# Single-row DMAs for two more kinds of chunk: the weighted sum and the sort of a graph network kernel on one core

## The reference, cut to what matters

```python
def _L0_gnn_ref(h, e, src, dst, W, b):          # "wsum": weighted sum of gathered rows
    m = h[src] * e
    ft = jax.ops.segment_sum(m, dst, num_segments=N_NODES)
    return ft @ W.T + b

def _L1_gnn_ref(x, edge_index, edge_attr, u, batch, W1, b1, W2, b2):   # "pool": needs edges by source
    row = edge_index[0]
    seg_sum = jax.ops.segment_sum(edge_attr, row, num_segments=N)
    seg_max = jax.ops.segment_max(edge_attr, row, num_segments=N)
    ...
# then _L2 ("rel": rows of hw[etype, src] summed by dst) and _L3 ("att": softmax over dst, rows z[src])
```

## Time and profile before

| what | value |
|---|---|
| median of 3 runs | 16717.06 us (16714.53 to 16719.4) |
| profiled execution: time, span | 16717.65 us, 16715.9 us |
| POOL busy | 12576.4 us, 75% of the span |
| DVE, ACT, PE busy | 50%, 16%, 12% |
| mean granted TensorE clock | 0.579 |

### The profile page before, as it was taken

The page is one execution under the profiler, slowest core; times in us unless marked ns, Lnnn a source line. Parts: engine busy times, 40 slices in busy tenths (PEclk is TensorE's granted clock), DMA queues, the critical chain, the costliest instruction groups (busy, mean ns, idle before and its releaser), DMA issues. The chain is left out here.

```text
span 16715.9 us, 114264 instructions
## 1 busy us (share of the span) xinstructions
PE 2071.2 (12%) x17217; PEld 1933.7 (12%) x17217; DVE 8380.9 (50%) x5953; ACT 2611.6 (16%) x1261; POOL 12576.4 (75%) x13194
## 2 busy tenths in 40 slices
PE   1212333333333111101320000000000000000000
PEld 1212333333323100101210000000000000000000
DVE  7878988888888677777621111111131222222222
ACT  0000111110101232232221111111110110111101
POOL 7777777777777777777767777777777777777776
PEclk9998666666666555555565555555555555555555
DMA  4222211112121233333532222222233222222222
GB/s 80 55 53 68 71 64 63 68 61 70 61 70 61 89 112 114 108 114 108 103 101 56 56 51 56 56 56 51 56 54 41 57 57 52 57 57 57 52 57 56
DMA packets 686784, 1141.43 MB, mean 68 GB/s; under 512 B 407713, under 2 KB 459500, under 8 KB 644044
## 3 DMA queue, kind: packets, MB, share of 16 engines
q0 software_dynamic: 421952, 380.03, 12.4%
q1 hardware_dynamic: 209740, 325.53, 6.6%
q10 hardware_dynamic: 54336, 428.56, 6.4%
HBM read 613.30 MB, written 519.84 MB: 68 GB/s over the span
## 5 line engine op out<-in xcount | busy, mean ns | idle before, releaser
L1079 POOL DMA_INDIRECT by_src<-H,sort_place_i x3224 | 3122.1, 968 | 983.7 <-issue 983.1
L559 POOL DMA_INDIRECT rel_G<-rel_table,rel_idx x3118 | 2945.7, 945 | 984.6 <-issue 951.3
L559 POOL DMA_INDIRECT att_G<-att_table,att_idx x3118 | 2942.2, 944 | 951.3 <-issue 951.3
L559 POOL DMA_INDIRECT lead_rows<-h_table,wsum_idx x3044 | 2887.2, 948 | 927.7 <-issue 927.7
L753 DVE SCALAR_TENSOR_TENSOR rel_Gf<-rel_Sf,rel_keep_first,rel_Gf 128x64 f32<-128x64 f32 x55 | 18.7, 341 | 3386.3 <-ACT rel_Gf L884 3386.3
L727 DVE TENSOR_TENSOR_SCAN att_near<-att_near,er_in 128x60 f32<-128x60 f32 (+2 forms) x55 | 19.3, 351 | 2835.1 <-issue 1846.7
L1247 PE MATMUL pG<-sort_cnt,sort_lowT 128*128 128x98 f32 x6448 | 1116.0, 348 | 816.7 <-DVE sort_prod L1137 816.7
L1247 PEld LDWEIGHTS pG<-sort_cnt,sort_lowT 128*128 128x128 f32 x6448 | 1071.6, 261 | 824.9 <-DVE sort_prod L1137 824.9
L951 PE MATMUL wsum_C<-wsum_high,wsum_low 128*128 128x98 fp8e4 x6448 | 560.9, 282 | 3369.2 <-DVE wsum_high L604 3369.2
L951 PEld LDWEIGHTS wsum_C<-wsum_high,wsum_low 128*128 128x128 fp8e4 x6448 | 520.1, 142 | 3410.6 <-issue 3410.6
L603 DVE TENSOR_TENSOR wsum_low<-iota_b,wsum_parts 128x3840 fp8e4<-128x3840 bf16 x216 | 891.7, 4128 | 9.8 <-DVE wsum_parts L594 9.8
(11 more groups left out here) (368 smaller groups left out, 7624.2 us busy)
## 6 DMA issues: line engine op xcount, KB each, us to landing
rel_G<-rel_table SPq DMA_DIRECT2D x8480, 0.2 KB
att_G<-att_table SPq DMA_DIRECT2D x8480, 0.3 KB
scan_att<-att_S ACTq DMA_DIRECT2D x53, 1980.0 KB
scan_wsum<-wsum_S ACTq DMA_DIRECT2D x53, 1920.0 KB, 6.5
sort_keys<-key_rows SPq DMA_DIRECT2D x53, 1920.0 KB, 9.6
scan_rel<-rel_S ACTq DMA_DIRECT2D x53, 1920.0 KB
scan_pool<-pool_S ACTq DMA_DIRECT2D x70, 1440.0 KB
rel_G<-rel_table ACTq DMA_DIRECT2D x5088, 0.2 KB
```

The lines of the kernel that those rows point to most:

```text
L559: pool.indirect_dma_start(out=G[s][:, j, :], out_offset=None, in_=table, in_offset=bass.IndirectOffsetOnAxis(ap=idx[s][:, j:j + 1], axis=0 ...
L1079: pool.indirect_dma_start(out=by_src, out_offset=bass.IndirectOffsetOnAxis(ap=place_i[s][:, j:j + 1], axis=0), in_=row[s][:, j, :], in_off ...
```

## The change

`COLUMNS` becomes 2 for the weighted sum and for the sort too, so POOL's share of each full chunk there falls from 60 columns to 58 (chunk 0 keeps 60). The 256 rows that are left go by single-row DMAs: in the weighted stages 160 by SP and 96 by ACT, in the sort 144 by SP and 112 by ACT. For the sort the byte addresses of the two columns are made by DVE (`place_bytes`), and each chunk's go out to DRAM and back into one partition by two small DMAs of SP that now stand among its loads for the next chunk. ACT issues its 112 rows of chunk k-1 in chunk k behind the first snapshot. The loads of `pool_row` move from SP to ACT. At the start of the first weighted stage ACT waits for the moved addresses and issues chunk 1's rows before it copies chunk 2's indices.

```diff
-    COLUMNS = dict(wsum=0, sort=0, rel=2, att=2)
-    BY_SP = dict(wsum=0, rel=160, att=160)
+    COLUMNS = dict(wsum=2, sort=2, rel=2, att=2)
+    BY_SP = dict(wsum=160, sort=144, rel=160, att=160)
...
                     if raw:
                         act.wait_ge(raw_var_ready, 1)
                         nc.scalar.activation(raw_root[:], raw_var[:], ACT.Sqrt).then_inc(raw_root_ready, 1)
+                        single.await_moved(act)
+                        act_rows_of_chunk(1)
...
                         act.wait_ge(pscanned, k + 2)
+                        if k + 1 < NC:
+                            load_rows(k + 1, SHORT if k + 1 == NC - 1 else SIDE)
...
                         if pooled:
                             number_following(i, s)
                             turn_pooled(2 * i + s)
+                            act_rows_of_chunk(c0 + 2 * i + s + 2)
                         own(i, s)
                         if pooled:
                             take_pooled(2 * i + s)
-                        act_rows_of_chunk(c0 + 2 * i + s + 2)
+                        else:
+                            act_rows_of_chunk(c0 + 2 * i + s + 2)
...
+                def issue_rows(engine, k, s, rows, landed):
...
+                    for r0 in range(rows.start, rows.stop, BATCH):
+                        registers = [engine.alloc_register(f"sort_row{k}_{r}") for r in range(r0, r0 + BATCH)]
+                        engine.load(registers, place_row[s][:, r0:r0 + BATCH])
+                        for r, register in enumerate(registers, r0):
...
+                            engine.dma_start(to[:, bass.ds(place, wide)], of[p:p + 1, at:at + wide]).then_inc(landed[k % TURNS], 16)
...
                         sp.wait_ge(place_ready, k + 1)
                         sp.sem_inc(loading, 1)
+                        if k:
+                            store_places(k - 1, 1 - s)
                         sp.dma_start(lows[:].unsqueeze(1), every_low[:, bass.ds(k, 1), :]).then_inc(lows_loaded, 16)
+                        if k:
+                            load_places(k - 1, 1 - s)
                         sp.dma_start(keys[:].unsqueeze(1), earlier_keys[:, bass.ds(k, 1), :]).then_inc(keys_loaded, 16)
...
                             if j == L // 4 and n is not None:
                                 pool.wait_ge(scattered[1 - s], 16 * (L - COLUMNS["sort"]) * n)
+                                pool.wait_ge(scattered_sp_rows[(k - 1) % TURNS], 16 * len(sort_by_sp) * ((k - 1) // TURNS + 1))
+                                if sort_by_act:
+                                    pool.wait_ge(scattered_act_rows[(k - 1) % TURNS], 16 * len(sort_by_act) * ((k - 1) // TURNS + 1))
                                 pool.sem_inc(rows_used, 1)
...
+                            for m in range(SC):
+                                j = L - SC + m
+                                v.tensor_scalar(place_bytes[s][:, m:m + 1], place[s][:, j:j + 1], rank[:, j:j + 1], float(4 * (A + 1)), ALU.add, ALU.mult)
...
                             snapshot(k * STEPS + g, s * STEPS + g)
+                            if g == 0 and k == 0:
+                                lead_single.issue(act, lead_chunk, range(BY_SP["wsum"], COLUMNS["wsum"] * P), lead["rows"][1][:], h_table, lead["act_rows"])
+                            if g == 0 and k and sort_by_act:
+                                act.wait_ge(places_moved, 32 * k)
+                                act.wait_ge(rows_ready, k + 2)
+                                issue_rows(act, k - 1, 1 - s, sort_by_act, scattered_act_rows)
```

More of the change, by code:

```diff
@@ L196, in build @@
                     gathered=[semaphore(f"lead_gathered{s}") for s in range(2)],
-                    sp_rows=[semaphore(f"lead_sp_rows{q}") for q in range(TURNS)] if COLUMNS["wsum"] else [])
-        scattered_rows = [semaphore(f"scattered_rows{q}") for q in range(TURNS)] if COLUMNS["sort"] else []
+                    sp_rows=[semaphore(f"lead_sp_rows{q}") for q in range(TURNS)],
+                    act_rows=[semaphore(f"lead_act_rows{q}") for q in range(TURNS)])
+        sort_by_sp, sort_by_act = range(0, BY_SP["sort"]), range(BY_SP["sort"], COLUMNS["sort"] * P)
+        scattered_sp_rows = [semaphore(f"scattered_sp_rows{q}") for q in range(TURNS)]
+        scattered_act_rows = [semaphore(f"scattered_act_rows{q}") for q in range(TURNS)] if sort_by_act else []
         scattered = [semaphore(f"scattered{s}") for s in range(2)]
@@ L412, in gathered_layer @@
                 sp_rows = lead["sp_rows"] if counts else [sem(f"sp_rows{q}") for q in range(TURNS)] if by_sp else []
-                act_rows = [sem(f"act_rows{q}") for q in range(TURNS)] if by_act else []
+                act_rows = lead["act_rows"] if counts else [sem(f"act_rows{q}") for q in range(TURNS)] if by_act else []
                 def await_rows(engine, i, s, w=L):
@@ L839, in _, with act_rows_of_chunk @@
                         nc.scalar.copy(idx[s][:], index[:, (c0 + s) * L:(c0 + s + 1) * L]).then_inc(index_ready, 1)
+                    def act_rows_of_chunk(k):
+                        if by_act and k < FULL:
+                            act.wait_ge(turned, k - c0 + 1)
+                            single.issue(act, k, by_act, G[k % 2][:], table, act_rows)
                     if raw:
@@ L895, in own @@
                                           S[s][:, 0:w, :]).then_inc(stored[s], 16)
-                    def act_rows_of_chunk(k):
-                        if by_act and k < FULL:
-                            act.wait_ge(turned, k - c0 + 1)
-                            single.issue(act, k, by_act, G[k % 2][:], table, act_rows)
                     def own_and_pooled(i, s):
@@ L909, in own_and_pooled @@
                             take_pooled(2 * i + s)
-                        act_rows_of_chunk(c0 + 2 * i + s + 2)
-                    for k in range(2):
-                        act_rows_of_chunk(c0 + k)
+                        else:
+                            act_rows_of_chunk(c0 + 2 * i + s + 2)
+                    if not counts:
+                        for k in range(2):
+                            act_rows_of_chunk(k)
+                    if pooled:
+                        await_scattered()
+                        load_rows(0)
                     for i in range(0, NC // 2 - 1):
@@ L1013, in scatter_by_source @@
                                      "based", "snapped", "updated", "summed", "picked", "placed", "place_ready", "issuing"))
-                if COLUMNS["sort"]:
-                    place_bytes = [sb(f"sort_place_bytes{s}", [P, 1], I32, c) for s in range(2)]
-                    place_row = [sb(f"sort_place_row{s}", [1, P], I32, c) for s in range(2)]
-                    places_moved = sem("places_moved")
+                SC = COLUMNS["sort"]
+                spare = free[:, -(-(2 * RW + WAYS * HT) // 64) * 64:].bitcast(I32)
+                place_row = [spare[0:1, s * SC * P:(s + 1) * SC * P] for s in range(2)]
+                place_bytes = [spare[:, (2 * P + s) * SC:(2 * P + s + 1) * SC] for s in range(2)]
+                places_moved = sem("places_moved")
+                def issue_rows(engine, k, s, rows, landed):
+                    wide = 4 * (A + 1)
+                    of = row[s].rearrange("p j f -> p (j f)").bitcast(U8)
+                    to = by_src.rearrange("n f -> (n f)").unsqueeze(0).bitcast(U8)
+                    for r0 in range(rows.start, rows.stop, BATCH):
+                        registers = [engine.alloc_register(f"sort_row{k}_{r}") for r in range(r0, r0 + BATCH)]
+                        engine.load(registers, place_row[s][:, r0:r0 + BATCH])
+                        for r, register in enumerate(registers, r0):
+                            n, p = r // P, r % P
+                            at = (L - SC + n) * wide
+                            place = engine.snap(register, donate=True, min_val=0, max_val=wide * (EP + 1))
+                            engine.dma_start(to[:, bass.ds(place, wide)], of[p:p + 1, at:at + wide]).then_inc(landed[k % TURNS], 16)
                 block = phase(c)
```

67 lines of the change are left out of this document (29 added, 38 removed).

## The result

The changed kernel takes 17047.72 us (median of 4 runs, 17035.15 to 17064.16) where the kernel before takes 16717.44 us in the same session: 1.0198 times as long, interval 1.0181 to 1.0216. The forecast was 16640 us, with a range up to 16760 us.

A forecast was written before the change was run, and what follows sets the result against it. POOL was taken to bound every gathering stage. First weighted stage -16, sort +19 and second weighted stage -81 made -78 us, so 16717.65 - 78 = 16640 us, range 16555 to 16760 us.

The forecast's parts named there:

- SP issues the store of places at T0 + 0.3, it lands in about 2 us, ... ACT is let go at T0 + 6: Sort: counted from a write of places (T0), store and load back let ACT start its rows after 6 us.
- it decides from 78.3 us a chunk: Rival, slower than before: places' load behind SP's queue traffic, T0 + 8.7, chunk 79.5 us, 16780 us; chance 0.16.
- upper bound of 81 us a chunk: Sort: addresses behind the keys too and SP's 0.434 us a row end ACT's blocking at T0 + 59.6.
- The rest of the sort's sum: Sort: ACT's 112 rows 49.2 us, then snapshot, PE and DVE work up to the next places; chunk 76.8 us.
- Each us of it is worth 52 us: Sort: each us of the chunk time, taken as 76.8 us, counts 52 us in the kernel.
- All of POOL's relief comes out: Rival: 265 us of relief less 31 us at two stage starts, 16484 us, ACT's blocking over by T0 + 52; chance 0.10.
- Start: First weighted stage: late addresses and indices leave POOL standing 29 us (bounds 20 to 38); stage -45 + 29 = -16 us.
- without this cover it would be up to 25 us: First weighted stage: SP's late rows cost nothing, as POOL may be two chunks ahead of DVE; otherwise up to 25 us.
- Second weighted stage: POOL loses 66 columns, -83 us, about 2 us late at start: -81 us; ACT's chunk 71 us, under POOL's 72.7.
- SP 69.4: Weighted stages: SP's 160 rows at rel's 0.434 us each take 69.4 us a chunk, fitting under POOL's 72.7.

The follow-up runs named there:

- q_after: Changed kernel with POOL nearly silent, one column a chunk in the sort and second weighted stage: 23868.57 us, ratio 0.9888 to the kernel before.
- q_direct: Changed kernel with POOL nearly silent and places moved straight into the row on one partition, without DRAM: 23289.59 us, ratio 0.9648 to the kernel before.
- c2_mid: Changed kernel with places moved without DRAM, chunk 2's indices copied before the address wait, pool_row loaded between pooled halves: 16567.21 us, 0.9887 of the kernel before.
- n0_none: Kernel before, complete, without any single rows (POOL takes all 60 columns in rel and att too): 19770.33 us, ratio 0.8189 on chip 7.

## Why the prediction was wrong

- **The step that failed is "SP issues the store of places at T0 + 0.3, it lands in about 2 us, ... ACT is let go at T0 + 6".** It took the landing from four transfers of 128 words that read DRAM. This one writes 256 neighbouring words, and it needs 8 to 10 us; then SP waits 4 to 6 us more for the load back. ACT is let go at about T0 + 15 (83.9 - 47.7 - 21.5), a chunk is 83.9 us in place of 76.8, and the sort got 400.6 us longer where I had 19. I had the rival ("it decides from 78.3 us a chunk", 16780 us) but looked for the delay in the queue and not in the writes, and stopped it at T0 + 8.7; it came true in its direction, not in its reason; my upper bound of 81 us a chunk was too low by 3. The row that bore on it was in front of me: the address move in front of rel, 50.8 us, "mostly a wait for single words to be written". I used it at the start, where it was right, and not in the sort.
- The rest of the sort's sum held: ACT's 112 rows with their register loads took 47.7 us (49.2 forecast), and 21.5 to 21.8 us stand behind them (21.6). "Each us of it is worth 52 us": q_after against q_direct gives 577 us for 10.9 us a chunk, 53 per us.
- "All of POOL's relief comes out" is, in the sort, nearly what c2_mid does: ACT's blocking was affordable once it began in time. It was not small: 112 rows held ACT 46.4 us in the changed kernel and 46.7 in q_after, and without them the loop was 9.9 us shorter. The Trainium skill, DMA: Bandwidth & Descriptors, section "Issuing engines are not separate DMA queues", says that the time to initiate a DMA is usually small relative to the DMA. Taken for 112 DMAs in turn, as that rival took it, the rule doesn't hold here; for a single row these traces give no landing to compare.
- Start: right. Addresses at 156 us and indices at 198 forecast, ACT's first row at 156.65 and the indices at 195.81 measured; POOL stood 21.9 us of the 29, as it came to the wait at 175 and not 169. Right in mechanism: POOL's gap, and that it costs 20 to 38 us. But that SP is late with its rows I had costed at nothing, "without this cover it would be up to 25 us". In c2_mid, with ACT's wait gone, POOL stood 20.7 us for it. In the changed kernel ACT's wait hid it, so the number was right in part by luck.
- Second weighted stage: the gather gave 67 of 81 us. The half's store behind the `pool_row` load cost 4 us (325.8 / 36 = 9.1 against 5.3), I had taken 3, and one chunk of ACT's took 71.6 us (7151.26 to 7222.81) where I had 71; POOL waited 9.2 us for ACT in all. What I costed wrongly is SP: "SP 69.4" from rel's 0.434 us a row, where in this stage it is 0.4645. So "SP 69.4" is 74.3, above POOL's 72.7; by the trace that is the 36 us at the end.

## What to carry to other kernels

A loop of engines that has slack takes a blocked sequencer well, but what counts is when the block starts: price the whole way of the data that it waits for, by a row of the same kind (writes by writes, in the same pattern), before pricing the block. Words that one engine hands to another's registers went quickest here from SBUF to SBUF, next 64 bytes or more apart through DRAM. Take an engine's issue rate from the stage where it will issue, and distrust a cover of 5% of the bound: 69.4 against 72.7 us was one, and it was gone.

## What the hardware showed unexpectedly

- 256 words of 4 bytes, neighbours in DRAM, were landed 8 to 10 us after the issue; 64 or 512 bytes apart 1.7 to 2 us; to one partition of SBUF about 2 us, an estimate (rows start at T0 + 3.5, a register load of 1.3 us included). What unit of memory is behind it, and whether 32 bytes would do, was not tried.
- The chips seem not to be alike. Chips 3, 4, 6 and 7 ran the kernel before at 24140 to 24223 us, chip 5 at 16752. Chips 4 and 7 were slow in both of the sessions that each had, and chip 5 had a single one between them. That it is the chip and not the hour is likely, but not shown. On chip 7 76 rows that ACT issued took 83.3 us; with POOL nearly silent the pace on such a chip was the normal one (q_after on chip 3: ACT's 112 rows in 46.7 us). So rows that pass beside POOL's indirect transfers are what waits, and PE's matmuls beside them do too, by the same 2.80 us. The single rows of rel and att, 106 x 2 columns by 1.25 us, should gain some 265 us on chip 5 (an estimate) and cost 4373 us on chip 7 (n0_none against the kernel before).
